# A graph block on one core: second-half one-hots made by GpSimd and ScalarE, and a transposed first layer of the experts

## The chip, the cores and the metric

The kernel runs on one NeuronCore of a Trainium2 chip. The metric is the device time of one execution in microseconds; before the change it is 5100.03 us, the median of three runs (5099.64 to 5103.68). The core's engines each work through a queue of their own in order and meet only at semaphores: TensorE (PE; its weight loads are shown as PEld), VectorE (DVE), ScalarE (ACT), GpSimd (POOL) and SyncE (SP, which here only starts DMAs).

## The reference, cut to what matters

A graph of 6250 nodes with 256 features and 106250 edges, sorted by their target node:

```
xn = layernorm(x)
h  = relu(tconv(xn));  g = tconv(h)             # two graph layers, 4 heads of 64
    tconv: kj = k[src] + e;  vj = v[src] + e;  e = edge_attr @ We
           logits = (q[dst] * kj).sum(head) / 8
           a = softmax of logits over the edges of one dst
           out = segment_sum(vj * a, dst) + x @ Ws + bs
x  = x + g + linear_attention(xn)
z  = layernorm(layernorm(x)) * gamma + beta     # the experts' own layer norm
y  = sum over the 2 best of 8 experts e: w_e * (gelu(z @ W1[e] + b1[e]) @ W2[e] + b2[e])
out = x + y                                     # W1[e]: 256x512, W2[e]: 512x256, all float32
```

## The kernel before

Stages run one after the other, with a barrier between them: `plan`, `nodes` of layer 1, `mix`, `edges` of layer 1, `nodes` and `edges` of layer 2, `finish`, `route`, `dispatch`, `experts`, `combine`. The change is in two of them.

**The edge stage.** The edges are cut into NS = 880 tiles of 128 edges, and each tile belongs to one block of 128 target nodes. T = 20 tiles make a chunk, NS / T = 44 chunks a layer; a chunk has two halves of HT = 10 tiles. Each engine has its own program over the same (chunk c, tile j), written out by hand: four chunks peeled, then a loop of ten chunks a turn. In what follows q = j // 2, since VectorE takes two tiles at once.

- SP loads the edge attributes `ea` of each tile, and the bytes `kb` from which the transposed one-hot `oht` is made.
- GpSimd (lines 859 to 870) gathers for each tile the rows of `kvD` at the edges' sources by an indirect DMA into `kv`, a ring of ten tiles. For each even j it waits first until VectorE has made the `vj` of the pair that last used these slots (`s_vj`). It also zeroes accumulator blocks (L859) and copies ten columns of indices each half chunk (L864).
- TensorE (L927, L931) computes for tile j the edge term `e` and the query of the targets (one-hot `oht` times `q`) into `ps`, four banks. After that, for the tile that lies LAG = 36 behind, it multiplies the one-hot `oh` with the weighted tile `w` into `pa` (L950). For this product it waits for `w` of the same j and for the `add` two tiles earlier. At j == 5 it transposes the logits of the chunk before (L936), at j == 13 it transposes the softmax's shifts (L941) and forms factors (L942).
- VectorE in a pair q: `add` of `pa` into the accumulator for j (L984), `kj` = kv + e (L1030), `vj` = kv + e (L1042), `add` for j + 1, `prod` = kj * query (L1062), the sum over a head (L994). At q = 2 to 5 stand the scans of the running maximum of a softmax. At q == 0 and q == 5 stands the one-hot `oh` of ten tiles, one `is_equal` of 128x1280 (L974): at q == 0 the one with m = 2c - 3 into half 1, at q == 5 the one with m = 2c - 2 into half 0. TensorE uses the latter from j == 16 of chunk c to j == 5 of chunk c + 1.
- ScalarE makes `w` for (c, j), the tile 36 behind: four scaled copies of a head (L909) and one of the weights (L911). `w` has four slots, so it runs at most four tiles ahead of TensorE's L950. Between them stand `keyed`, Abs and Relu that make `oht` from `kb` (L883, L885), at j == 4 and j == 14, and the exponentials at j == 15.

**The experts.** Nodes are sorted by expert into NE = 108 tiles of 128 rows (a multiple of 6; 105 suffice). For each tile: two transposes of x (L1499), a copy to SBUF by ScalarE (L1537), the first layer with x as the stationary operand and W1 moving, 512 columns (L1508), bias by VectorE (L1565), gelu by ScalarE (L1543), four transposes of the result (L1517), a copy by ScalarE (L1549), the second layer (L1526), bias by VectorE (L1573), a store. Each engine runs the steps of several tiles interleaved (`piped`: step (d, f) does f for the tile d turns back). The expert's number is read into a register from a table. GpSimd has nothing to do here.

Of the kernel before, what the change touches and what calls it, by code (L numbers as in the profile page):

```python
# [32 lines left out]
EX = 8  # L33
# [23 lines left out]
def sizes(n_nodes, n_edges):  # L57

    z = Record()
    z.N, z.E = n_nodes, n_edges  # L60
    z.NB = -(-n_nodes // P)
    z.NT = -(-n_edges // P)
    z.NT += -(z.NT + z.NB - 1) % 40
    z.NS = z.NT + z.NB - 1
    z.NSP = -(-z.NS // P) * P
    z.U = z.NSP // P
    z.G = z.NSP // 32
    z.NE = -(-(2 * z.NB + EX - 1) // 6) * 6
    z.UB = max(d for d in range(1, 8) if z.NB % d == 0)
    return z  # L70
# [669 lines left out]
def edges(nc, z, g, layer, a):  # L740
# [3 lines left out]
    with Stage(nc, f"edge{layer}") as st:  # L744
# [42 lines left out]
        s_resc, s_vinit, s_off, s_abs = (st.sem(n) for n in ("s_resc", "s_vinit", "s_off", "s_abs"))  # L787
# [56 lines left out]
        def _(pool):  # L844
# [32 lines left out]
        def _(act):  # L877
# [37 lines left out]
        def _(pe):  # L915
# [38 lines left out]
        def _(dve):  # L954
# [42 lines left out]
            def chunk(c, k0, u, kept, more):  # L997
# [9 lines left out]
                for q in range(HT):  # L1007
# [65 lines left out]
                    if j % HT == 0 and lagged(c, j + 6):  # L1073
                        onehot(2 * c - (3 if j < HT else 2), 1 if j < HT else 0)
# [197 lines left out]
def route(nc, z, g, a):  # L1272
# [4 lines left out]
    with Stage(nc, "route") as st:  # L1277
# [163 lines left out]
def experts(nc, z, g, a):  # L1441
# [3 lines left out]
    with Stage(nc, "exp") as st:  # L1445
        xr = st.sb("xr", [P, UE, D])
        xT = st.sb("xT", [P, 2, D])
        hb = st.sb("hb", [P, 2, HID])
        hg = st.sb("hg", [P, 2, HID])
        hT = st.sb("hT", [P, 2, HID])  # L1450
        yo = st.sb("yo", [P, UE, D])
        pX = st.ps("pX", [P, 2, 2 * D])
        pH = st.ps("pH", [P, 2, HID])
        pT = st.ps("pT", [P, 2, HID])
        pY = st.ps("pY", [P, 2, 2 * D])
        s_tx, s_xT, s_h, s_hb, s_hg, s_th, s_hT, s_y, s_yo = (
            st.sem(n) for n in ("s_tx", "s_xT", "s_h", "s_hb", "s_hg", "s_th", "s_hT", "s_y", "s_yo"))
# [5 lines left out]
        def piped(eng, stages):  # L1463
# [11 lines left out]
            for j in range(deep):  # L1475
                for d, f in stages:
                    if j < d:
                        f(n_turns - 1, j - d + UE)

        @block.sync  # L1480
        def _(sp):
            def body(i):
                for j in range(UE):
                    t = i * UE + j
                    need(sp, s_tx, t - UE + 1)
                    sp.dma_start(xr[:, j, :], g.xsD[bass.ds(t * P, P), :]).then_inc(s_x[j], 16)
            turns(sp, n_turns, body)

        @block.tensor
        def _(pe):  # L1490
# [11 lines left out]
            def first(i, j):  # L1502
                t = i * UE + j
                e = expert(t)
                pe.wait_ge(s_xT, t + 1)
                need(pe, s_hb, t - 1)
# [5 lines left out]
            def h_transpose(i, j):  # L1512
                t = i * UE + j
                pe.wait_ge(s_hg, t + 1)
                need(pe, s_hT, t - 1)
                for c in range(KH):
                    ins = nc.tensor.transpose(pT[:, j % 2, c * P:(c + 1) * P], hg[:, j % 2, c * P:(c + 1) * P], g.ident[:, :])  # L1517
                ins.then_inc(s_th, 1)
# [10 lines left out]
            piped(pe, ((0, x_transpose), (1, first), (2, h_transpose), (3, second)))  # L1529

        @block.scalar
        def _(act):
            def x_copy(i, j):
                t = i * UE + j
                act.wait_ge(s_tx, t + 1)
                need(act, s_h, t - 1)
                nc.scalar.activation(xT[:, j % 2, :], pX[:, j % 2, 0:D], ACT.Copy).then_inc(s_xT, 1)  # L1537

            def gelu(i, j):
                t = i * UE + j  # L1540
                act.wait_ge(s_hb, t + 1)
                need(act, s_th, t - 1)
                nc.scalar.activation(hg[:, j % 2, :], hb[:, j % 2, :], ACT.Gelu).then_inc(s_hg, 1)  # L1543

            def h_copy(i, j):
                t = i * UE + j
                act.wait_ge(s_th, t + 1)
                need(act, s_y, t - 1)
                nc.scalar.activation(hT[:, j % 2, :], pT[:, j % 2, :], ACT.Copy).then_inc(s_hT, 1)  # L1549
# [4 lines left out]
            piped(act, ((0, x_copy), (1, gelu), (2, h_copy), (4, store)))  # L1554
            for j in range(UE):
                act.wait_ge(s_st[j], 16 * n_turns)

        @block.vector
        def _(dve):
            def bias1(i, j):  # L1560
                t = i * UE + j
                e = dve.value_load(g.etab[0:1, bass.ds(t, 1)], min_val=0, max_val=EX - 1)
                dve.wait_ge(s_h, t + 1)
                need(dve, s_hg, t - 1)
                nc.vector.tensor_tensor(hb[:, j % 2, :], pH[:, j % 2, :], g.b1[:, bass.ds(e, 1), :].rearrange("p o n -> p (o n)"),  # L1565
                                        ALU.add).then_inc(s_hb, 1)
# [8 lines left out]
            piped(dve, ((1, bias1), (3, bias2)))  # L1575
# [70 lines left out]
def build(nc, z, a, out):  # L1646
# [24 lines left out]
    with ExitStack() as whole:  # L1671
# [28 lines left out]
        g.b1 = keep(whole, "b1", [P, EX, HID])  # L1700
# [42 lines left out]
```

## Time and profile before

| | |
|---|---|
| median of 3 runs | 5100.03 us |
| the profiled execution | 5088.28 us, its span 5086.5 us |
| PE busy | 4248.3 us, 84% |
| PEld busy | 3321.2 us, 65% |
| DVE busy | 3889.5 us, 76% |
| ACT busy | 2768.2 us, 54% |
| POOL busy | 2630.0 us, 52% |

Edge stages fill about 480 to 2150 us and 2440 to 4092 us of the span, the experts 4475 to 4920 us. Each row of a timeline gives start, duration, engine, line and operation, and in brackets how long the engine had stood idle before and who released it. Matmuls of one group are merged into one row with their count; their ends overlap the next group's start, since they are pipelined. Two float32 instructions belong to one matmul of the program.

### The profile page before, as it was taken

How to read it: one execution, taken by the hardware profiler on the slowest of the kernel's cores; microseconds unless marked ns; L12 is line 12 of the kernel's file. 1: busy time of each engine (PE TensorE's matmuls, PEld its weight loads, DVE VectorE, ACT ScalarE, POOL GpSimd, SP SyncE). 2: the span in 40 equal slices, each digit the busy share in tenths (PEclk: the TensorE clock that was granted, in tenths of full speed). 3: DMA queues.
4: the chain of work that ended last, by engine and by line, in shares of the span. 5: the costliest groups of instructions: out<-in, count | busy, mean ns of one | idle time of the engine just before them, and what ended most of it. 6: DMA issues, size and time to landing. Idle time of an engine off the chain costs nothing. (4 is left out here: it accounts for less than half of the span.)

```text
span 5086.5 us, 105694 instructions
## 1 busy us (share of the span) xinstructions
PE 4248.3 (84%) x18414; PEld 3321.2 (65%) x18415; DVE 3889.5 (76%) x8471; ACT 2768.2 (54%) x10075; POOL 2630.0 (52%) x2743
## 2 busy tenths in 40 slices
PE   2987999999999999878999999999999933089960
PEld 1555788788788788633788788788788722056640
DVE  3444999999999999944999999999999976022222
ACT  0120677777777777711577777777777721033320
POOL 1011777677677677400777767767677523600015
PEclk9998999999999999989999999999999955589985
DMA  4457877777777777444877777777777623422225
GB/s 84 137 197 218 234 218 215 210 217 216 213 214 218 209 216 220 136 138 141 253 215 218 218 210 218 217 212 215 213 216 216 169 87 139 161 67 64 64 89 153
DMA packets 617242, 923.33 MB, mean 182 GB/s; under 512 B 114469, under 2 KB 478565, under 8 KB 616390
## 3 DMA queue, kind: packets, MB, share of 16 engines
q0 software_dynamic: 154544, 502.26, 34.6%
q1 hardware_dynamic: 378822, 325.73, 22.8%
q10 hardware_dynamic: 83280, 89.03, 5.0%
q14 instruction: 422, 3.46, 0.2%
q8 instruction: 174, 2.85, 0.2%
HBM read 803.36 MB, written 113.31 MB: 180 GB/s over the span
## 5 line engine op out<-in xcount | busy, mean ns | idle before, releaser
L870 POOL DMA_INDIRECT edge_kv<-kvD,edge_ix x1760 | 1819.1, 1034 | 937.2 <-issue 431.0
L909 ACT ACTIVATE edge_w<-edge_vj,edge_ex 128x64 f32<-128x64 f32 x7040 | 1865.4, 337 | 631.9 <-PE edge_pa L950 615.7
L927 PE MATMUL edge_ps<-edge_We,edge_ea 112*128 112x256 f32 x7040 | 1838.9, 383 | 47.1 <-DVE edge_prod L1062 25.2
L927 PEld LDWEIGHTS edge_ps<-edge_We,edge_ea 112*128 112x128 f32 x7040 | 1323.9, 190 | 289.5 <-DVE edge_prod L1062 55.8
L950 PE MATMUL edge_pa<-edge_w,edge_oh 128*128 128x260 f32 x3520 | 1094.6, 393 | 116.6 <-DVE acc L984 91.4
L931 PE MATMUL edge_ps<-acc,edge_oht 128*128 x3520 | 1056.5, 381 | 0.5 <-ACT edge_oht L885 0.5
L950 PEld LDWEIGHTS edge_pa<-edge_w,edge_oh 128*128 128x128 f32 x3520 | 619.2, 189 | 316.2 <-ACT edge_w L911 177.4
L984 DVE TENSOR_TENSOR acc<-acc,edge_pa 128x260 f32 x1760 | 730.4, 415 | 91.4 <-PE edge_pa L950 45.7
L931 PEld LDWEIGHTS edge_ps<-acc,edge_oht 128*128 128x128 f32 x3520 | 674.0, 192 | 96.1 <-issue 1.9
L1030 DVE TENSOR_TENSOR edge_kj<-edge_kv,edge_ps 128x512 f32<-128x512 f32 x880 | 597.9, 679 | 39.9 <-PE edge_ps L931 20.9
L1062 DVE TENSOR_TENSOR edge_prod<-edge_kj,edge_ps 128x512 f32<-128x512 f32 x880 | 597.5, 679 | 0.0
L1042 DVE TENSOR_TENSOR edge_vj<-edge_kv,edge_ps 128x512 f32<-128x512 f32 x880 | 596.1, 677 | 0.0
L994 DVE TENSOR_REDUCE edge_Lc<-edge_prod 128x8 f32<-128x512 f32 x880 | 595.8, 677 | 0.0
L859 POOL COPY acc<-edge_zero 128x1040 f32 x440 | 469.5, 1067 | 36.6 <-DVE edge_vj L1042 32.4
L468 PE MATMUL nodes_pj<-nodes_W,nodes_xT 128*128 128x512 f32 x784 | 364.7, 610 | 26.8 <-ACT nodes_xT L409 26.8
L883 ACT ACTIVATE edge_oht<-edge_kb,edge_npart 128x1280 f32<-128x1280 uint8 x178 | 240.0, 1348 | 192.0 <-POOLq L869 104.7
L911 ACT ACTIVATE edge_w<-edge_ex 128x4 f32<-128x4 f32 x1760 | 343.4, 195 | 0.0
L1565 DVE TENSOR_TENSOR exp_hb<-exp_pH,b 128x512 f32<-128x512 f32 x108 | 74.7, 692 | 324.7 <-PE exp_pH L1508 324.7
L974 DVE TENSOR_TENSOR edge_oh<-free,relS 128x1280 f32<-128x1280 f32 x176 | 268.2, 1524 | 0.0
L468 PEld LDWEIGHTS nodes_pj<-nodes_W,nodes_xT 128*128 128x128 f32 x784 | 145.2, 195 | 182.6 <-issue 146.6
L1605 POOL COPY comb_ix<-pos 128x14 int32 (+1 forms) x7 | 1.4, 196 | 485.5 <-POOLq L86 462.0
L885 ACT ACTIVATE edge_oht<-edge_oht,ones 128x1280 f32<-128x1280 f32 x178 | 242.5, 1362 | 5.8
(230 smaller groups left out, 3140.3 us busy)
## 6 DMA issues: line engine op xcount, KB each, us to landing
edge_ea<-ea_t_dram SPq DMA_DIRECT2D x1760, 112.0 KB, 4.1
edge_kb<-relD SPq DMA_DIRECT2D x178, 160.0 KB, 4.4
edge_kv<-kvD,edge_ix POOLq DMA_INDIRECT x1760, 4.4
kvD<-nodes_kvs ACTq DMA_DIRECT2D x98, 256.0 KB, 2.1
xsD<-mix_zr POOLq DMA_DIRECT2D x27, 512.0 KB
exp_xr<-xsD SPq DMA_DIRECT2D x108, 128.0 KB, 2.0
ysD<-exp_yo ACTq DMA_DIRECT2D x108, 128.0 KB
edge_pen<-penD SPq DMA_DIRECT2D x352, 32.0 KB
```

Of the source, the lines that this page charges most:

```text
L468: ins = nc.tensor.matmul(pj[:, j % 2, n * 2 * D:(n + 1) * 2 * D], xT[:, j, c, :], W[:, c, n * 2 * D:(n + 1) * 2 * D], start=(c == 0), stop ...
L859: nc.gpsimd.tensor_copy(g.acc[:, bass.ds(block + 1, AHEAD - 1), :].rearrange("p b n -> p (b n)"), zero[:, 0:1].to_broadcast([P, (AHEAD - 1 ...
L870: nc.gpsimd.indirect_dma_start(out=kv[:, j % HT, :], out_offset=None, in_=g.kvD, in_offset=bass.IndirectOffsetOnAxis(ap=ix[:, h, j % HT:j ...
L909: nc.scalar.activation(w[:, j % 4, h * CA:h * CA + C], vj[:, slot, h * C:(h + 1) * C], ACT.Copy, scale=ex[:, x, h, k:k + 1])
L927: nc.tensor.matmul(ps[:, j % 4, 0:D], ea[:, j % HT, k, :], We[:, k, :], start=(k == 0), stop=(k == 1))
L931: nc.tensor.matmul(ps[:, j % 4, D:2 * D], oht[:, j // HT, (j % HT) * P:(j % HT + 1) * P], g.q[:, bass.ds(block, 1), 0:D].rearrange("p o d ...
L950: nc.tensor.matmul(pa[:, j % 2, 0:A], oh[:, par, (j + 4) % HT, :], w[:, j % 4, :], start=True, stop=True).then_inc(s_ape, 1)
L984: nc.vector.tensor_tensor(at, at, pa[:, j % 2, 0:A], ALU.add).then_inc(s_acc, 1)
L994: nc.vector.tensor_reduce(Lc[:, p, :, s:s + 2].rearrange("p h s -> p s h"), prod[:, q % 2, :, :].rearrange("p s (h k) -> p s h k", h=H), A ...
L1030: nc.vector.tensor_tensor(kj[:, q % 2, :, :], kv[:, both, 0:D], e, ALU.add).then_inc(s_kj, 1)
L1042: nc.vector.tensor_tensor(vj[:, p * T + j:p * T + j + 2, :], kv[:, both, D:2 * D], e, ALU.add).then_inc(s_vj, 1)
L1062: nc.vector.tensor_tensor(prod[:, q % 2, :, :], kj[:, q % 2, :, :], ps[:, bank, D:2 * D], ALU.mult).then_inc(s_prod, 1)
```

## The change

Edge stage: the one-hot with even m (half 0 of `oh`) is no longer made by VectorE. GpSimd subtracts (free index minus the edge's target, 128x1280) at j == 1 of its chunk c for m = 2c - 4, and ScalarE makes Abs and then Relu(1 - x) of it in place at j == 12 of its chunk c, for m = 2c - 2. `keyed` for the next chunk moves from j == 14 to j == 16.

Experts: the first layer is computed transposed. The W1 of the tile's expert is copied by GpSimd into `Ws` (two slots) and is the stationary operand, in blocks of 128 x 128; x transposed is moving, 128 columns. Its result has the hidden units on partitions, so the four transposes and their copy fall away, and `b1` becomes the bias of the gelu activation. The copy of x from PSUM goes from ScalarE to VectorE. NE is 105.

```diff
-    z.NE = -(-(2 * z.NB + EX - 1) // 6) * 6
+    z.NE = 2 * z.NB + EX - 1
 # edges, gpsimd
+            def offsets(m, par):
+                need(pool, s_ape, HT * m - HT)
+                nc.gpsimd.tensor_tensor(oh[:, par, :, :], g.free[:, :].unsqueeze(1).to_broadcast([P, HT, P]),
+                                        g.relS[:, bass.ds(m * HT, HT)].unsqueeze(2).to_broadcast([P, HT, P]), ALU.subtract).then_inc(s_off, 1)
             def chunk(c, k0, u, kept, more):
                 for j in range(T):
+                    if j == 1 and (not isinstance(c, int) or 2 <= c <= NCH + 1):
+                        offsets(2 * c - 4, 0)
 # edges, scalar
+            def onehot(done, par):
+                act.wait_ge(s_off, done)
+                nc.scalar.activation(oh[:, par, :, :], oh[:, par, :, :], ACT.Abs).then_inc(s_abs, 1)
+                act.wait_ge(s_abs, done)
+                nc.scalar.activation(oh[:, par, :, :], oh[:, par, :, :], ACT.Relu, bias=g.ones[:, 0:1], scale=-1.0).then_inc(s_ohs, 1)
             def chunk(c, k0, u, kept, more):
                 for j in range(T):
+                    if j == 12 and lagged(c, 16):
+                        onehot(c, 0)
-                    if j == 14 and (not isinstance(c, int) or c + 1 < NCH):
+                    if j == 16 and (not isinstance(c, int) or c + 1 < NCH):
                         keyed(2 * c + 2, c + 1, 0)
 # edges, tensor
-                            pe.wait_ge(s_oh, 2 * c - (2 if j < HT else 1))
+                            pe.wait_ge(*((s_oh, c - 1) if j < HT else (s_ohs, c)))
 # edges, vector
-                    if j % HT == 0 and lagged(c, j + 6):
-                        onehot(2 * c - (3 if j < HT else 2), 1 if j < HT else 0)
+                    if j == 0 and lagged(c, 6):
+                        onehot(2 * c - 3, 1)
 # experts, gpsimd (new)
+            def stage(i, j):
+                t = i * UE + j
+                e = pool.value_load(g.etab[0:1, bass.ds(t, 1)], min_val=0, max_val=EX - 1)
+                need(pool, s_h, t - 1)
+                nc.gpsimd.tensor_copy(Ws[:, j % 2, :, :].rearrange("p c n -> p (c n)"),
+                                      g.W1[:, bass.ds(e, 1), :, :].rearrange("p o c n -> p (o c n)")).then_inc(s_ws, 1)
 # experts, tensor, first layer
-                for c in range(2):
-                    ins = nc.tensor.matmul(pH[:, j % 2, :], xT[:, j % 2, c * P:(c + 1) * P],
-                                           g.W1[:, bass.ds(e, 1), c, :].rearrange("p o n -> p (o n)"), start=(c == 0), stop=(c == 1))
+                for m in range(KH):
+                    for c in range(2):
+                        ins = nc.tensor.matmul(pH[:, j % 2, m * P:(m + 1) * P],
+                                               Ws[:, j % 2, c, m * P:(m + 1) * P],
+                                               xT[:, j % 2, c * P:(c + 1) * P], start=(c == 0), stop=(c == 1))
-            piped(pe, ((0, x_transpose), (1, first), (2, h_transpose), (3, second)))
+            piped(pe, ((0, x_transpose), (1, first), (2, second)))
 # experts, scalar
+                for m in range(KH):
+                    ins = nc.scalar.activation(hT[:, j % 2, m * P:(m + 1) * P], pH[:, j % 2, m * P:(m + 1) * P], ACT.Gelu,
+                                               bias=g.b1[:, bass.ds(e, 1), m])
-            piped(act, ((0, x_copy), (1, gelu), (2, h_copy), (4, store)))
+            piped(act, ((1, gelu), (3, store)))
 # experts, vector
-            piped(dve, ((1, bias1), (3, bias2)))
+            piped(dve, ((0, x_copy), (2, bias2)))
```

The rest of the diff is the loading of `b1` in its new layout and the last, incomplete turn of the experts' loop.

## Rows read from the trace of the kernel before

**Rows 1.** The page: its first line.
```profile
span 5086.5 us, 105694 instructions
```

**Rows 2.** Five chunks of edge layer 2: L974 by tile (durations min/median/max, starts); busy by engine.
```profile
L974 DVE TENSOR_TENSOR edge_oh<-free,relS x11: 1478/1481/1915, 3007.7 to 3193.8; 128x1280 f32<-128x1280 f32 x11
...
3007.67:3193.80 186.13, 180.64 (x822) 150.93 (x821) 182.90 (x386) 140.48 (x531) 131.73 (x134) 1.00 0.76 216
```

**Rows 3.** Timeline of TensorE, one chunk (start us, us, engine line op).
```profile
3001.53 1.03 PE L927 MATMUL edge_ps<-edge_We,edge_ea 112*128 112x256 f32 x4
...
3010.21 1.03 PE L927 MATMUL edge_ps<-edge_We,edge_ea 112*128 112x256 f32 x4
...
3011.51 0.27 PE L936 MATMUL edge_pm<-ident,edge_Lc 128*128 128x128 f32 x1
...
3022.01 0.60 PE L931 MATMUL edge_ps<-acc,edge_oht 128*128 x2
...
3024.18 0.62 PE L950 MATMUL edge_pa<-edge_w,edge_oh 128*128 128x260 f32 x2
...
3026.05 0.28 PE L942 MATMUL edge_pm<-edge_Ym,ones 128*128 128x4 f32 x2
```

**Rows 4.** Timeline of VectorE, the same chunk: q = 0, then q = 5.
```profile
3004.95 0.68 DVE L1030 TENSOR_TENSOR edge_kj<-edge_kv,edge_ps 128x512 f32<-128x512 f32 x1
...
3023.90 0.68 DVE L1030 TENSOR_TENSOR edge_kj<-edge_kv,edge_ps 128x512 f32<-128x512 f32 x1
...
3024.83 0.68 DVE L1042 TENSOR_TENSOR edge_vj<-edge_kv,edge_ps 128x512 f32<-128x512 f32 x1
...
3027.77 1.48 DVE L974 TENSOR_TENSOR edge_oh<-free,relS 128x1280 f32<-128x1280 f32 x1
```

**Rows 5.** Timeline of ScalarE, the same chunk: j = 12 and j = 14.
```profile
3017.57 1.07 ACT L909 ACTIVATE edge_w<-edge_vj,edge_ex 128x64 f32<-128x64 f32 x4 [0.67 <-PE edge_pa L950]
...
3020.58 1.34 ACT L883 ACTIVATE edge_oht<-edge_kb,edge_npart 128x1280 f32<-128x1280 uint8 x1
3021.96 1.36 ACT L885 ACTIVATE edge_oht<-edge_oht,ones 128x1280 f32<-128x1280 f32 x1
3023.23 1.05 ACT L909 ACTIVATE edge_w<-edge_vj,edge_ex 128x64 f32<-128x64 f32 x4
```

**Rows 6.** Timeline of GpSimd: the next chunk's gather for j = 0.
```profile
3026.31 0.96 POOL L870 DMA_INDIRECT edge_kv<-kvD,edge_ix  x1 [1.59 <-DVE edge_vj L1042]
```

**Rows 7.** GpSimd's operations by line: durations in ns, min/median/max.
```profile
L1176 POOL TENSOR_TENSOR fin_xg<-fin_xn,fin_gam x49: 717/724/901, 4115.7 to 4277.3; 128x256 f32<-128x256 f32 x49
...
L859 POOL COPY acc<-edge_zero x440: 1051/1058/1704, 497.6 to 4058.0; 128x1040 f32 x147
...
L864 POOL COPY edge_ix<-srcS x176: 189/201/1521, 478.3 to 4021.2; 128x10 int32 x160, 128x10 int32<-128x10 int32 x16
```

**Rows 8.** TensorE at edge layer 1's start: timeline; a window (PE busy, clock, DMA share, GB/s).
```profile
481.71 2.05 PE L927 MATMUL edge_ps<-edge_We,edge_ea 112*128 112x256 f32 x4 [8.11 <-DMA edge_ea<-ea_t_dram]
...
485.89 0.60 PE L931 MATMUL edge_ps<-acc,edge_oht 128*128 x2
...
480.00:485.00 5.00, 3.29 (x7) 0.50 0.77 216
```

**Rows 9.** TensorE: one tile of the experts; L465's 128-column matmuls of 100 us (PE, PEld busy).
```profile
4703.63 1.88 PE L1508 MATMUL exp_pH<-W,exp_xT 128*128 x4
4705.35 0.60 PE L1517 MATMUL exp_pT<-ident,exp_hg 128*128 128x128 f32 x4
4705.79 1.89 PE L1526 MATMUL exp_pY<-W,exp_hT 128*128 x8
...
4707.73 1.88 PE L1508 MATMUL exp_pH<-W,exp_xT 128*128 x4
...
200.00:300.00 100.00, 22.40 (x168) 20.63 (x168) 1.00 0.39 132
```

**Rows 10.** ScalarE in the experts: the gelu of 512 columns.
```profile
4706.39 0.63 ACT L1543 ACTIVATE exp_hg<-exp_hb 128x512 f32<-128x512 f32 x1 [2.17 <-DVE exp_hb L1565]
```

More of the change, by code:

```diff
@@ L786, in edges @@
         s_oh, s_w, s_ape, s_acc, s_init = (st.sem(n) for n in ("s_oh", "s_w", "s_ape", "s_acc", "s_init"))
-        s_resc, s_vinit, s_off, s_abs = (st.sem(n) for n in ("s_resc", "s_vinit", "s_off", "s_abs"))
+        s_resc, s_vinit, s_off, s_abs, s_ohs = (st.sem(n) for n in ("s_resc", "s_vinit", "s_off", "s_abs", "s_ohs"))
         s_mt, s_m, s_D, s_et, s_ex, s_Y = (st.sem(n) for n in ("s_mt", "s_m", "s_D", "s_et", "s_ex", "s_Y"))
@@ L1474, in piped @@
             turns(eng, n_turns, body, peel=2)
-            for j in range(deep):
+            for t in range(n_turns * UE, NE + deep):
                 for d, f in stages:
-                    if j < d:
-                        f(n_turns - 1, j - d + UE)
+                    if t - d < NE:
+                        f((t - d) // UE, (t - d) % UE)
         @block.sync
@@ L1485, in body, with _ @@
                     need(sp, s_tx, t - UE + 1)
-                    sp.dma_start(xr[:, j, :], g.xsD[bass.ds(t * P, P), :]).then_inc(s_x[j], 16)
+                    if not isinstance(t, int) or t < NE:
+                        sp.dma_start(xr[:, j, :], g.xsD[bass.ds(t * P, P), :]).then_inc(s_x[j], 16)
             turns(sp, n_turns, body)
+            body(n_turns)
+        @block.gpsimd
+        def _(pool):
+            def stage(i, j):
[4 more added lines that the diff above has]
+                                      g.W1[:, bass.ds(e, 1), :, :].rearrange("p o c n -> p (o c n)")).then_inc(s_ws, 1)
+            piped(pool, ((0, stage),))
         @block.tensor
@@ L1503, in first @@
                 t = i * UE + j
-                e = expert(t)
                 pe.wait_ge(s_xT, t + 1)
-                need(pe, s_hb, t - 1)
-                for c in range(2):
-                    ins = nc.tensor.matmul(pH[:, j % 2, :], xT[:, j % 2, c * P:(c + 1) * P],
-                                           g.W1[:, bass.ds(e, 1), c, :].rearrange("p o n -> p (o n)"), start=(c == 0), stop=(c == 1))
-                ins.then_inc(s_h, 1)
[L1512 to L1518, printed above, removed]
+                pe.wait_ge(s_ws, t + 1)
+                need(pe, s_hT, t - 1)
+                for m in range(KH):
[3 more added lines that the diff above has]
+                                               xT[:, j % 2, c * P:(c + 1) * P], start=(c == 0), stop=(c == 1))
+                ins.then_inc(s_h, 1)
             def second(i, j):
@@ L1553, in store, with x_copy @@
                 act.dma_start(g.ysD[bass.ds((i * UE + j) * P, P), :], yo[:, j, :]).then_inc(s_st[j], 16)
-            piped(act, ((0, x_copy), (1, gelu), (2, h_copy), (4, store)))
+            piped(act, ((1, gelu), (3, store)))
             for j in range(UE):
-                act.wait_ge(s_st[j], 16 * n_turns)
+                act.wait_ge(s_st[j], 16 * -(-(NE - j) // UE))
         @block.vector
         def _(dve):
-            def bias1(i, j):
+            def x_copy(i, j):
                 t = i * UE + j
[L1562 to L1566, printed above, removed]
+                dve.wait_ge(s_tx, t + 1)
+                need(dve, s_h, t - 1)
+                nc.vector.tensor_copy(xT[:, j % 2, :], pX[:, j % 2, 0:D]).then_inc(s_xT, 1)
             def bias2(i, j):
@@ L1734 @@
         lay[n] = np.asarray(inputs["L0_ffn_" + n])
+    lay["b1_T"] = np.ascontiguousarray(lay.pop("b1").reshape(EX, HID // P, P).transpose(2, 0, 1))
     nc = bacc.Bacc("TRN2", target_bir_lowering=False, num_devices=1)
```

26 lines of the change are left out of this document (7 added, 19 removed).

## The prediction

> **What bounds the kernel now.** I read the page first: its 40 slices show two long plateaus (the edge stage of each graph layer) in which TensorE and VectorE both stand at nine tenths or more, and near the end a short stretch where TensorE alone does. The span is 5086.5 us [rows 1]. Then I asked for busy time in a stretch of exactly five chunks inside the second plateau. The `is_equal` one-hot of VectorE comes twice a chunk, and ten intervals of it take 186.1 us, so a chunk of 20 tiles takes 37.2 us; in that stretch VectorE is busy 182.90 of 186.13 us and TensorE 180.64 [rows 2]. Next come the timelines of the engines in one chunk, since shares cannot say who waits for whom.
>
> TensorE [rows 3]: from the first row to the second are 5 tiles in 8.68 us, 1.736 us a tile, 34.7 us a chunk. The transpose of `Lc` and the group at j == 13 (last row) add at most their own 0.27 and 0.28 us, together about 0.5. So TensorE alone needs 35.2 us a chunk and now loses 2.0 to waits. VectorE [rows 4]: the pairs from q = 0 to q = 5 take 3004.95 to 3023.90, 18.95 us, where TensorE needs 5 x 3.47 + 0.1 = 17.5. So VectorE falls behind by 1.5 us here and sets the pace; it makes that up in the second half of the chunk, were it not for the one-hot at q = 5, 1.48 us, which is the one the change takes away. VectorE is the bound by a thin margin, TensorE stands 2.0 us behind it.
>
> ScalarE [rows 5] makes the weighted tile `w` of a j up to four tiles before TensorE multiplies it: `w` of j = 12 starts at 3017.57 (released by TensorE's j = 8), and TensorE takes it at 3024.18 [rows 3]. GpSimd [rows 6] runs ahead too, but only by the ten slots of `kv`: its gather for j = 0 of the next chunk starts at 3026.31, after a wait for VectorE's `vj` of q = 5, which ended at 3024.83 + 0.68 = 3025.51 [rows 4].
>
> **Edit 1, the one-hot of each second half.** Removed: 1.48 us of VectorE a chunk. Added: a subtract on GpSimd (`offsets`), Abs and Relu on ScalarE (`onehot`). What decides is their place in two queues. `offsets(2c-2)` stands at j == 1 of GpSimd's chunk c+1, behind the gather of j = 0 of that chunk. ScalarE waits for that very subtract (`s_off >= c`) at j == 12 of chunk c, ahead of `w` for j = 12. TensorE needs that `w` for the product of j = 12, before it does anything else. So every chunk gets a chain, begun when `vj` of q = 5 ends (call it V):
>
> - to the start of the gather 0.80 us (3025.51 to 3026.31), the gather 0.96 [rows 4, 6];
> - the subtract, 128x1280, two SBUF inputs. The trace has none of that size. The nearest row is GpSimd's 128x256 multiply, 717 ns [rows 7]. Above: five of these, 3.6 us. Below: the rate of GpSimd's one-input copy, 1.058 us for 1040 columns, gives 1.3 us. A copy of ten columns takes 0.20, so some 0.2 of the 717 ns is fixed; (0.717 - 0.2) x 5 + 0.2 = 2.8 us. I take 2.8, as the multiply has the two inputs;
> - to ScalarE, an estimate of 0.1; Abs to Relu 1.38 (3020.58 to 3021.96), Relu to the next `w` 1.27 (to 3023.23), `w` itself 1.05 for four heads and about 0.1 for its tail [rows 5]; to TensorE an estimate of 0.1.
>
> Sum: 0.80 + 0.96 + 2.8 + 0.1 + 1.38 + 1.27 + 1.15 + 0.1 = 8.6 us after V. Meanwhile everything stops: TensorE in order at the product of j = 12; VectorE after the rest of q = 5, as `add` of j = 12 needs that product; GpSimd after two gathers, as the next need `vj` of q = 6.
>
> The new period, from one product of j = 12 to the next: TensorE's own chunk 35.2, less what lies between the end of the products of j = 11 into `ps` (3022.01 + 0.60 = 3022.61) and the product of j = 12 (3024.18) [rows 3], 1.57, makes 33.6. Add 0.2 for waits on `add` that stay (an estimate, a tenth of the 2.0 lost now, since VectorE now follows). Add the clock: where TensorE had stood 8.11 us it came back at a granted clock of 0.50, and L927, L931, L927 took 4.18 us from 481.71 to 485.89 [rows 8], against 0.87 + 0.43 + 0.87 = 2.17 at full clock [rows 3]: 2.0 lost. The stall here is longer (below), so I add 2.0. Then V after TensorE's j = 11: the lag of 1.5 us that VectorE gathers from q = 0 to q = 5, and kj to the end of `vj`, 3023.90 to 3025.51, 1.6 [rows 4]; 3.1. Then the chain, 8.6. Sum 33.6 + 0.2 + 2.0 + 3.1 + 8.6 = 47.5 us against 37.2: 10.3 more a chunk. TensorE stands 3.1 + 8.6 - 1.57 = 10.1 us in each. VectorE's saved 1.48 us buys nothing; its cover was the chunk's critical path, which has moved.
>
> That clock loss draws on one gap of the trace. The Trainium skill ("TensorE: Matmul & The Clock Gate", section "HAM oscillation — how this bites in real kernels") says that a kernel whose every loop turn has such a gap pays the slow start in every turn. By that rule the 2.0 us belongs in all chunks, without it the period is 45.5 us; only the one gap here bears it out.
>
> How often: NS / T = 44 chunks a layer. c = 2 to 42 have it in full. c = 43: GpSimd's chunk 44 has no gathers, the subtract can start some 1.2 us sooner. c = 1 has nothing queued before j = 16, and TensorE reaches that four tiles later; Relu ends 3.1 - 1.15 us or so later than needed with keyed and `w` behind it, about 3.5 us. c = 44 and the tail: nothing to gather, no stall, one one-hot less. Per layer 42 x 10.3 - 1.2 + 3.5 - 1.4 = 434, two layers +868 us.
>
> keyed moved from j == 14 to j == 16: two ScalarE activations, 2.65 us [rows 5], needed by TensorE only at j = 0 of the next chunk. After the stall ScalarE does `w` of 12 to 15 at about 1.15 us each while TensorE needs 1.74 or more, so I cost it at nothing; if that cover were gone it would cost up to 1 us a chunk.
>
> **Edit 2, the experts.** Now TensorE works without a gap, 4703.63 to 4707.73, 4.10 us a tile, 108 tiles, 443 us [rows 9]. Removed: the four transposes of `hg`, 4705.35 to 4705.79, 0.44 us; three tiles of padding, 12 us. The first layer goes from 4 instructions of 512 columns (4703.63 to 4705.35, 1.72) to 16 of 128. Groups of eight such products, with as many weight loads, stand in the node stage: 168 take 22.40 us, 21 groups of 1.067 [rows 9], in which the last product's tail is about 0.17, so 0.112 each. 16 x 0.112 = 1.79, 0.07 more. New tile 4.10 - 0.44 + 0.07 = 3.73; 105 x 3.73 = 392: -51 us. Bounds: as 16 x 0.107 it is -58; were every load exposed by as much as a product, 16 x 0.11 = 1.8 a tile, +138.
>
> Added and hidden: GpSimd's copy of the expert's weights, 1024 columns, near the 1.06 us of 1040 [rows 7], or with the multiply's rate 2.1; it has from the end of `first(t-2)` to `first(t)`, one and a half tiles, 5.5 us. ScalarE: four gelus of 128 columns in place of three activations; a 512-wide one takes 0.63 [rows 10], so four cost between 0.63 and 2.5 of the 3.73. The copy of `x` goes to VectorE, which loses `bias1`. Register loads of the expert number on GpSimd and ScalarE are not in the trace; at under 1 us they stay covered, if not the copy's cover is gone by their excess. SP's queue: the same loads, three fewer; ScalarE's stores likewise. `b1` is loaded as 4 columns an expert; the route stage ends on VectorE's chain, so nothing.
>
> **Sum.** 5088.3 (profiled execution, 5086.5 and 1.8 around) + 868 - 51 = 5905 us. The median of the runs shown is 12 us above it, which I add: 5917.
>
> **Rivals.**
> 1. No clock loss: a stall of 10 us does not lower the clock every time. 5917 - 2 x 42 x 2.0 = 5750. For it: in the long plateau the clock is 1.00. Against: the 8.11 us gap.
> 2. Not slower. The chain ends before TensorE wants `w` of j = 12, because GpSimd is further ahead than in the rows. Then VectorE's load falls to 37.2 - 1.4 = 35.8, TensorE's 35.2, and the period is some 35.6: -1.6 x 88 = -141, with the experts 5100 - 192 = 4908. It decides from a subtract that starts 10.1 us earlier, three pairs of gathers. GpSimd is idle a quarter of the time, but the ring of ten `kv` slots holds it, so the row of 3026.31 speaks against.
> 3. The experts' weight loads are exposed: 5917 + 51 + 138 = 6106. The node stage's rows speak against.
> 4. The subtract runs at the copy's rate: 1.5 us less a chunk, 5917 - 126 = 5791; inside the range.
>
> **How the numbers follow.** My case, with 4 in it: 0.83. Rival 1: 0.07. Rival 2: 0.05. Rival 3: 0.03. The rest, a stall much shorter or something unseen, 0.02. The range takes in the subtract from 1.3 to 3.6 us (-126 to +67), an error of 1 us a chunk in lag and waits (84 either way), and rival 1: 5740 to 6060. About 0.2% is what a measurement tells from no change. Faster 0.06, same 0.01, slower 0.93.
>
> **What would show it.** In the edge stage after: a period near 47.5 us; TensorE's longest wait is `pa` <- `w` of ScalarE, near 10 us, once a chunk, about 84 times; ScalarE waits for GpSimd's `oh` from about where it now starts `w` of j = 12; the subtract stands right behind a gather released by `vj`; the first L950 and L927 after each stall take twice their time and the mean granted clock of the stage falls below 0.95. In the experts TensorE stays gapless at about 3.73 us a tile. I am wrong if `offsets` starts well ahead of `vj` of q = 5, or if TensorE finds `w` of j = 12 ready.

## The result and the profile after

The changed kernel takes 5946.29 us (median of 4 runs, 5939.01 to 5950.19) against 5101.85 for the kernel before on the same chip (5099.64 to 5105.57): ratio 1.1653, 95% interval 1.1632 to 1.1673. The profiled execution took 5945.37 us. I had forecast 5917 in a range of 5740 to 6060. Medians of the kernel before differ by half a per cent from one batch of runs to the next, on the same chip too (5076.44 and 5103.20 on one of them), so the experiments are compared as ratios, each to the kernel before in its own batch.

The page of the changed kernel: span and busy time by engine, granted clock in slices, the costliest groups (busy, mean ns | idle before, releaser); line numbers in the edge stage are 7 to 15 higher than before (L859 is L866, L870 is L877, L927 is L942, L950 is L965).

```profile
span 5943.0 us, 107412 instructions
PE 4414.9 (74%) x19200; PEld 3569.5 (60%) x19201; DVE 3782.1 (64%) x8377; ACT 2890.5 (49%) x10348; POOL 2870.4 (48%) x2936
PEclk9988888888888888889888888888888887558995
L965 PE MATMUL edge_pa<-edge_w,edge_oh 128*128 128x260 f32 x3520 | 1187.3, 422 | 808.5 <-ACT edge_w L926 796.9
L897 ACT ACTIVATE edge_oh<-edge_oh 128x1280 f32<-128x1280 f32 x88 | 111.7, 1269 | 1114.9 <-POOL edge_oh L852 1114.9
```

The span is 856.5 us longer [rows 1], VectorE has 107 us less to do, and no engine is above 74%: the time is not in work but in waits. The view of waits gives the links (waited for: us in total, times, longest):

```profile
ACT edge_oh L897 <- POOL edge_oh L852: 1114.9, 86, 25.6
PE edge_pa L965 <- ACT edge_w L926: 796.9, 120, 10.6
DVE acc L999 <- PE edge_pa L965: 711.9, 256, 7.9
```

ScalarE waits for GpSimd's subtract once a chunk, TensorE for ScalarE's `w`, VectorE for TensorE's product. One chunk on the four engines, VectorE first (`vj` of q = 5, then the next `add`):

```profile
3445.53 0.68 DVE L1057 TENSOR_TENSOR edge_vj<-edge_kv,edge_ps 128x512 f32<-128x512 f32 x1
...
3455.52 0.43 DVE L999 TENSOR_TENSOR acc<-acc,edge_pa 128x260 f32 x1 [7.32 <-PE edge_pa L965]
```

GpSimd, ending with the subtract:

```profile
3447.02 0.96 POOL L877 DMA_INDIRECT edge_kv<-kvD,edge_ix  x1 [1.59 <-DVE edge_vj L1057]
3448.00 2.34 POOL L852 TENSOR_TENSOR edge_oh<-free,relS 128x1280 f32<-128x1280 f32 x1
```

ScalarE, from the last `w` before the wait to the next:

```profile
3437.58 0.19 ACT L926 ACTIVATE edge_w<-edge_ex 128x4 f32<-128x4 f32 x1
3450.37 1.27 ACT L897 ACTIVATE edge_oh<-edge_oh 128x1280 f32<-128x1280 f32 x1 [12.60 <-POOL edge_oh L852]
3451.67 1.36 ACT L899 ACTIVATE edge_oh<-edge_oh,ones 128x1280 f32<-128x1280 f32 x1
3452.94 1.05 ACT L924 ACTIVATE edge_w<-edge_vj,edge_ex 128x64 f32<-128x64 f32 x4
```

TensorE: the last products into `ps` of j = 12, the product of j = 12 after its wait, and what follows.

```profile
3442.72 0.60 PE L946 MATMUL edge_ps<-acc,edge_oht 128*128 x2
...
3444.45 0.60 PE L946 MATMUL edge_ps<-acc,edge_oht 128*128 x2
3454.14 1.24 PE L965 MATMUL edge_pa<-edge_w,edge_oh 128*128 128x260 f32 x2 [9.09 <-ACT edge_w L926]
3455.16 1.91 PE L942 MATMUL edge_ps<-edge_We,edge_ea 112*128 112x256 f32 x4
```

`vj` ends at 3446.21, and the product starts at 3454.14: 7.93 us, in the order gather, subtract, Abs, Relu, `w`, as the arrows name them. After the wait L965 and the four matmuls of L942 take about twice what they take elsewhere (0.60 and 1.03): from 3454 to 3458 us the granted clock is 0.50, the lower of the two levels. It is so behind each of the 86 waits of this kind (medians 1.24 and 1.91). In the kernel before, GpSimd's same gather [rows 6] was followed at once by the next one (at 3027.58), and TensorE had its `w`.

The stages, by the start of their first instruction: the edge stage of layer 1 with the node stage behind it takes 2389.4 us (471.8 to 2861.2) where it took 1930.2 (477.2 to 2407.4), 459 more; the edge stage of layer 2 takes 2142.1 for 1687.7, 454 more; the experts take 402.7 for 452.5, 49.8 less. One tile of the experts, in the changed kernel (before: [rows 9]):

```profile
5600.76 1.95 PE L1533 MATMUL exp_pH<-exp_xT,exp_Ws 128*128 128x128 f32 x16
5602.54 1.89 PE L1544 MATMUL exp_pY<-W,exp_hT 128*128 x8
5604.27 0.38 PE L1523 MATMUL exp_pX<-ident,exp_xr 128*128 128x128 f32 x2
5604.49 1.73 PE L1533 MATMUL exp_pH<-exp_xT,exp_Ws 128*128 128x128 f32 x14
```

TensorE is gapless there, 3.73 us a tile.

### The profile page after: what moved, and what is told of

Read it like the earlier page. It is cut to its first block and busy times, and to the rows that moved or that the text cites. A ratio compares the mean times of both kernels' runs of the same rounds, so it can differ in the third digit from the quotient of the medians.

```text
span 5943.0 us, 107412 instructions
## 1 busy us (share of the span) xinstructions
PE 4414.9 (74%) x19200; PEld 3569.5 (60%) x19201; DVE 3782.1 (64%) x8377; ACT 2890.5 (49%) x10348; POOL 2870.4 (48%) x2936
## 3 DMA queue, kind: packets, MB, share of 16 engines
q14 instruction: 424, 3.47, 0.2%
## 5 line engine op out<-in xcount | busy, mean ns | idle before, releaser
L877 POOL DMA_INDIRECT edge_kv<-kvD,edge_ix x1760 | 1754.3, 997 | 1701.8 <-DVE edge_vj L1057 1208.7
L942 PE MATMUL edge_ps<-edge_We,edge_ea 112*128 112x256 f32 x7040 | 1933.9, 399 | 44.8 <-DVE edge_prod L1077 20.4
L965 PE MATMUL edge_pa<-edge_w,edge_oh 128*128 128x260 f32 x3520 | 1187.3, 422 | 808.5 <-ACT edge_w L926 796.9
L942 PEld LDWEIGHTS edge_ps<-edge_We,edge_ea 112*128 112x128 f32 x7040 | 1414.6, 202 | 309.2 <-issue 48.0
L965 PEld LDWEIGHTS edge_pa<-edge_w,edge_oh 128*128 128x128 f32 x3520 | 672.7, 203 | 985.9 <-ACT edge_w L926 849.2
L946 PE MATMUL edge_ps<-acc,edge_oht 128*128 x3520 | 1096.8, 393 | 0.5 <-issue 0.5
L946 PEld LDWEIGHTS edge_ps<-acc,edge_oht 128*128 128x128 f32 x3520 | 699.4, 199 | 107.5 <-issue 1.8
L897 ACT ACTIVATE edge_oh<-edge_oh 128x1280 f32<-128x1280 f32 x88 | 111.7, 1269 | 1114.9 <-POOL edge_oh L852 1114.9
L866 POOL COPY acc<-edge_zero 128x1040 f32 x440 | 467.0, 1061 | 46.1 <-DVE edge_vj L1057 41.9
L1557 ACT ACTIVATE exp_hT<-exp_pH,b 128x128 f32<-128x128 f32 x420 | 119.8, 368 | 267.4 <-PE exp_pH L1533 267.4
L1509 POOL COPY exp_Ws<-W 128x1024 f32 x105 | 109.2, 1040 | 289.8 <-PE exp_pH L1533 278.5
```

Source lines behind the costliest of these rows:

```text
L866: nc.gpsimd.tensor_copy(g.acc[:, bass.ds(block + 1, AHEAD - 1), :].rearrange("p b n -> p (b n)"), zero[:, 0:1].to_broadcast([P, (AHEAD - 1 ...
L877: nc.gpsimd.indirect_dma_start(out=kv[:, j % HT, :], out_offset=None, in_=g.kvD, in_offset=bass.IndirectOffsetOnAxis(ap=ix[:, h, j % HT:j ...
L942: nc.tensor.matmul(ps[:, j % 4, 0:D], ea[:, j % HT, k, :], We[:, k, :], start=(k == 0), stop=(k == 1))
L946: nc.tensor.matmul(ps[:, j % 4, D:2 * D], oht[:, j // HT, (j % HT) * P:(j % HT + 1) * P], g.q[:, bass.ds(block, 1), 0:D].rearrange("p o d ...
L965: nc.tensor.matmul(pa[:, j % 2, 0:A], oh[:, par, (j + 4) % HT, :], w[:, j % 4, :], start=True, stop=True).then_inc(s_ape, 1)
```

## The experiments

Period means the median of the 43 distances between two chunks' groups of j == 13 on TensorE in layer 1 (before: 37.07 us; changed kernel: 47.76). All kernels are the changed one with the edit shown.

| run | what it is | ratio to before | 95% | period |
|---|---|---|---|---|
| e1_edges_only | experts as before | 1.1794 | 1.1774 to 1.1813 | 47.71 |
| e2_experts_only | edge stage as before | 0.9912 | 0.9896 to 0.9929 | 37.05 |
| e10_experts_again | the same, again | 0.9898 | 0.9884 to 0.9912 | 37.06 |
| e3_scalar_at_16 | Abs and Relu at j == 16 | 1.005 | 1.0034 to 1.0067 | 37.50 |
| e5b_filler | 20 products in the wait | 1.128 | 1.1264 to 1.1296 | 44.95 |
| e6_subtract_twice | subtract doubled | 1.2013 | 1.1993 to 1.2033 | 49.79 |
| e8_copy_twice | copy of W1 doubled | one run, 5948.19 us | | 47.76 |
| e4_subtract_early | subtract at j == 15 | 0.9921 | 0.9903 to 0.9939 | 36.75 |
| e7_subtract_at_14 | subtract at j == 14 | 0.9888 | 0.987 to 0.9906 | 37.10 |
| e9_subtract_17_scalar_13 | subtract at 17, Abs at 13 | 1.0056 | 1.0044 to 1.0068 | 38.29 |
| e11_first_half | the other one-hot | 0.9932 | 0.9918 to 0.9945 | 36.86 |
| e12_first_half_6 | the same, subtract at j == 6 | 0.9821 | 0.9804 to 0.9838 | 36.44 |

### Which part costs

e1_edges_only takes back every experts hunk of the diff. 

> The edge edits alone, the experts as before. My theory: the loss is all in the edge stage, the experts give about 50 us back, so this is slower than the full change by 50: 5946 + 50 = 5996 us, ratio 1.175. The period of a chunk stays 47.4 to 47.8 us. Rival: the experts' edit costs something elsewhere (the weight loads, the copy on GpSimd) and the edges lose less; then this kernel is at or below 5946.

e2_experts_only takes back every edge-stage hunk. 

> The experts' edits alone, the edge stage as before. My theory: 5102 - 50 = 5052 us, ratio 0.990; the tile takes 3.74 us as in the changed kernel, 105 tiles. Rival: the two edits interact over the stage boundary (buffers, barriers), then this and the edges alone do not add up to the full change within 10 us.

Measured 1.1794 and 0.9912. Their effects add up nearly: 1.1794 + 0.9912 - 1 = 1.1706 against 1.1653, 0.5% apart, which is more than the intervals. The two batches differ by as much in the kernel before (5076.44 and 5101.85 us), and the changed kernel was not run in the first one; so whether the gap is one of batches or of the kernel stays open. The edge part costs the whole loss, the experts gain what was forecast.

### Is it the place in ScalarE's queue

```diff
-                    if j == 12 and lagged(c, 16):
-                        onehot(c, 0)
-                    if j == 16 and (not isinstance(c, int) or c + 1 < NCH):
+                    if j == 14 and (not isinstance(c, int) or c + 1 < NCH):
                         keyed(2 * c + 2, c + 1, 0)
+                    if j == 16 and lagged(c, 16):
+                        onehot(c, 0)
```

> The full change, but ScalarE's Abs and Relu stand at j == 16, right before TensorE needs that one-hot, and keyed stands at j == 14 as before. Theory A (the queue: w of j = 12 to 15 stands behind the wait for GpSimd): GpSimd's subtract still ends about 4.1 us after vj of q = 5, Relu 2.65 later, w of 16 at 7.9, TensorE is there at about 6.0, so a stall of about 2 us a chunk is left instead of 9.1, and with it the clock loss goes: period 37.2 to 38, total 5050 to 5120 us. Theory B (the chain from GpSimd is too late for TensorE in itself, whatever stands behind it; or the extra work on ScalarE and GpSimd is what costs): the period stays above 44 us and the total above 5600.

Measured 1.005, period 37.5. All the instructions of the change are still there, at the same lengths; only their order in ScalarE's queue is another: `w` of j = 12 to 15, `keyed` and the exponentials now stand ahead of the wait. Of the 796.9 us that TensorE waited for `w`, 149.9 are left, and of ScalarE's 1114.9 us 174.0. So the loss is the order of ScalarE's queue against GpSimd's, not the work moved.

### Two sizes of the chain: the clock and the subtract

```diff
+                        if j == 12:
+                            need(pe, s_ex, c - 1)
+                            for _ in range(20):
+                                nc.tensor.matmul(pm[:, 1, D + 8:2 * D], g.ident[0:EP, :], We[:, 0, 0:D - 8], start=True, stop=True)
```

> The full change, and TensorE, before it waits for w of j = 12, does 20 float32 products of 248 columns into an unused part of a PSUM bank (about 8.3 us of the 9.1 us stall; nothing uses their result). My theory, clock: in the stall the granted clock falls to 0.50, and the work after it loses 2.6 us a chunk. With the filler the clock stays 1.00, the first products after the stall take 0.6 us and not 1.24, the period falls from 47.7 to about 45.1, and the total by 86 x 2.6 = 224 us: ratio 1.165 - 0.044 = 1.121. Rival: the clock after the stall does not matter since VectorE or ScalarE sets the pace there: within 30 us of the changed kernel, ratio 1.16, or slower by what the filler overruns.

Measured 1.128. TensorE's timeline in it (the filler, then the product of j = 12):

```profile
3420.48 8.53 PE L965 MATMUL edge_pm<-edge_We,ident 112*128 112x248 f32 x40
3429.73 0.70 PE L969 MATMUL edge_pa<-edge_w,edge_oh 128*128 128x260 f32 x2 [0.72 <-ACT edge_w L926]
3430.28 1.03 PE L942 MATMUL edge_ps<-edge_We,edge_ea 112*128 112x256 f32 x4
```

The useless products fill the wait and 0.72 us of it remain; L942 takes 1.03 again where it took 1.91. From the end of `vj` of q = 5 to TensorE's product it is 7.93 us in both kernels (medians), so the chain is the same. The period falls by 47.76 - 44.95 = 2.8 us, and that is about what the clock cost in each chunk: a kernel that does more work is 3% faster. The Trainium skill ("TensorE: Matmul & The Clock Gate", section "HAM oscillation — how this bites in real kernels") says that a gap in each loop turn makes each turn pay the slow start; the trace agrees, with L942 at 1.91 us behind all 86 waits.

```diff
             def offsets(m, par):
                 need(pool, s_ape, HT * m - HT)
+                nc.gpsimd.tensor_tensor(spare[:, :, :], ...the same inputs..., ALU.subtract).then_inc(s_step, 1)
```

> The full change with a second GpSimd subtract of the same size into a spare tile, ahead of the real one. My theory: it lies on the chain that sets the period, so its 2.34 us come out in full, once a chunk: +2.34 to 2.45 x 85 = +200 us, 6145 us. Rival: GpSimd's own time is hidden and the stall has another cause (ScalarE's load, the clock): less than +50 us.

Measured 1.2013, 0.036 over the changed kernel, which is 183 us or 2.1 us in each of 88 chunks (the period: 2.03). The chain from `vj` to the product grows from 7.93 to 10.20 us: the second subtract of 2.34 us lands on the path nearly in full.

### The cover of the experts' copy

```diff
+                need(pool, s_wx, t)
+                nc.gpsimd.tensor_copy(Wx[:, :], g.W1[:, bass.ds(e, 1), :, :].rearrange("p o c n -> p (o c n)")).then_inc(s_wx, 1)
```

> The full change with GpSimd's copy of the expert's weights made twice, first into a spare tile. My theory: the copy is hidden, GpSimd stands idle 2.69 of 3.74 us a tile, so a second 1.04 us changes nothing: the tile stays 3.74 us, the experts' stage within 3 us. Rival: the copy is on the path, +1.04 us a tile, +109 us.

GpSimd does both copies in a tile (1.04 us each), and still waits for TensorE:

```profile
5602.90 1.04 POOL L1512 COPY exp_Wx<-W 128x1024 f32 x1 [1.71 <-PE exp_pH L1537]
5603.88 1.04 POOL L1513 COPY exp_Ws<-W 128x1024 f32 x1
```

The stage takes 402.7 us as in the changed kernel. The copy is hidden with room for another.

### Can the edge part pay

If the subtract starts early enough, the chain is off the path and rival 2's period, some 35.6 us, should come. Three runs tried the place:

```diff
-                    if j == 1 and (not isinstance(c, int) or 2 <= c <= NCH + 1):
-                        offsets(2 * c - 4, 0)
+                    if j == 15 and (not isinstance(c, int) or 1 <= c <= NCH):
+                        offsets(2 * c - 2, 0)
```

> The full change, but GpSimd does the subtract at j == 15 of chunk c, six tiles earlier in its queue than j == 1 of chunk c + 1; ScalarE stays at j == 12. Theory A (order in GpSimd's queue behind a gather released by vj of q = 5): the subtract now ends near the point at which ScalarE reaches j = 12, with w up to four tiles ahead, so nothing stalls; the chunk is bound by VectorE's 35.8 and TensorE's 35.2, period 35.8 to 36.4, against 37.1 before; total 5052 - 88 x (0.7 to 1.3) = 4940 to 4990 us, faster than both kernels. Theory B (the added 2.6 us of ScalarE and 2.3 of GpSimd a chunk cost by themselves, by delayed w or gathers): no better than 5052.

Measured 0.9921, period 36.75: missed, and no better than the experts alone. The stall is gone, but VectorE has a new long instruction. GpSimd, VectorE in the same stretch, then that scan over the whole run (ns, min/median/max):

```profile
3017.78 2.33 POOL L852 TENSOR_TENSOR edge_oh<-free,relS 128x1280 f32<-128x1280 f32 x1
```

```profile
3018.96 1.22 DVE L1053 TENSOR_TENSOR_SCAN edge_X<-edge_wp,edge_R,edge_TT 128x20 f32<-128x20 f32 x1
...
L1053 DVE TENSOR_TENSOR_SCAN edge_X<-edge_wp,edge_R,edge_TT x88: 253/1218/2922, 524.6 to 4062.7; 128x20 f32<-128x20 f32 x88
```

Before, the same scan took 255 ns. It ends at 3020.18, as the subtract does (3020.11): VectorE's instruction with two inputs in SBUF is held while GpSimd's runs, whereas `kj`, one of whose inputs is in PSUM, keeps its 0.68 us. So I moved the subtract one tile forward (`j == 14` for `j == 15`):

> As the subtract at j == 15, but one gather sooner, at j == 14. At j == 15 the period came out at 36.74 us: the subtract lay from 3017.78 to 3020.11, and VectorE's small scan at q = 3, both of whose inputs are in SBUF, took 1.22 us from 3018.96 instead of 0.26 and so ended with the subtract. Theory A (GpSimd's subtract holds what VectorE needs for an operation with two SBUF inputs): at j == 14 it ends near 16.8, before the scan, which takes 0.26 again; VectorE has 0.96 us a chunk less, period 35.8 to 36.0 us, total about 85 x 0.8 = 65 us under that of j == 15, ratio 0.977 to 0.982. Theory B (the period of 36.7 is set by something else, TensorE's add waits or ScalarE's extra work): period 36.6 to 36.8, ratio 0.992.

Measured 0.9888. The scan's median is 255 ns again, as expected, and the period is not below 37: missed, so the scan alone did not hold it. What VectorE waits for in five chunks of layer 2:

```profile
DVE edge_kj L1045 <- PE edge_ps L946: 7.0, 5, 1.7
```

In e2_experts_only this wait does not occur in that stretch. One of the five waits stands before q = 9, two before q = 8, two before q = 5; over the 82 full chunks of the run a wait of over 0.3 us stands before q = 8 in 30 and before q = 5 in 30. The third place was j == 17, with `onehot` on ScalarE at j == 13:

> The full change with GpSimd's subtract at j == 17 of chunk c and ScalarE's Abs and Relu at j == 13. From the trace of the subtract at j == 15: the subtract would lie from about 21.3 to 23.6 (the scan of q = 3 with two SBUF inputs is at 19.0, the next such scan at 26.0), Relu ends near 26.3, w of j = 13 near 27.5, and TensorE wants it at 29.1: no stall, no held scan, gathers 14 to 17 not delayed. Theory A (the two places were the only costs): period 35.8 to 36.2 us, 60 to 80 us under the experts' edits alone, ratio 0.976 to 0.981. Theory B (a third cost, which took the gain at j == 14: a gather that lands late once a subtract has held up GpSimd's queue): period 36.5 to 37, ratio 0.987 to 0.992.

Measured 1.0056: missed, by what looks like e4's reason again. GpSimd's zeroing COPY, pushed back by the subtract, now meets another of VectorE's scans with SBUF inputs (GpSimd and VectorE in one chunk, then the scan over the run):

```profile
3054.95 1.06 POOL L866 COPY acc<-edge_zero 128x1040 f32 x1
```

```profile
3054.84 1.46 DVE L1092 TENSOR_TENSOR_SCAN edge_B<-edge_pen,edge_GY,edge_F 128x128 f32<-128x128 f32 x1
...
L1092 DVE TENSOR_TENSOR_SCAN edge_B<-edge_pen,edge_GY,edge_F x88: 472/1460/1804, 530.3 to 4160.3; 128x128 f32<-128x128 f32 x88
```

It took 475 ns in the kernel before. How much of this run's 1.2 us a chunk over the kernel before the scan explains (1.0) rests on its length alone; no run separates it. The table further down shows the rest: beside the 1.0 of the scan, at q = 4, the pair of q = 7 is 1.4 us longer, by a wait for `ps`, which is all that the pair of q = 5 had saved. The control for e7:

> The experts' edits alone, run again beside the one above so that the two are compared on the same chip: ratio 0.990, period 37.05 us. Nothing else is asked of it.

Its interval overlaps that of e7, so up to here nothing showed a gain from the edge part.

### Where the saved time has to lie

e7 saves VectorE 1.4 us a chunk, and in that stretch of layer 2 VectorE waits 1.4 us a chunk for `ps`. That gave a new theory: VectorE falls behind TensorE from q = 0 to q = 5 (the scans) and catches up after that, 3.06 us a pair against 3.47. The one-hot of q = 5 stood where it catches up. Without it VectorE only catches up sooner, and waits. I had put all five waits before q = 8, where this holds; two stand before q = 5, and for those the theory has no reason. By it the one to take away is the other, at q = 0:

```diff
-                        offsets(2 * c - 4, 0)          # GpSimd, j == 1
+                        offsets(2 * c - 3, 1)          # GpSimd, j == 4
-                        onehot(c, 0)                   # ScalarE, j == 12; keyed at 4 and 16
+                        onehot(c - 1, 1)               # ScalarE, j == 2; keyed at 6 and 14
-                        onehot(2 * c - 3, 1)           # VectorE, q == 0
+                        onehot(2 * c - 2, 0)           # VectorE, q == 5
```

> The other one-hot is taken from VectorE: GpSimd and ScalarE make the one of odd m (subtract at j == 4 of GpSimd's chunk, Abs and Relu at j == 2 of ScalarE's, keyed back at 14 and its neighbour from 4 to 6); VectorE keeps the one of even m, at q == 5. The experts are as in the changed kernel. VectorE loses the same 1.48 us a chunk as in e7_subtract_at_14, but in the half in which it falls behind TensorE. Theory S (only what is saved while VectorE is behind counts; in the second half of a chunk it catches up with TensorE and then waits for ps, as the 7.0 us in five chunks before kj of q = 8 show in e7): the period falls by a further 0.9 to 1.4 us below the 36.9 of e7, to 35.5 to 36.0, no wait of VectorE before kj at q = 8, time 0.965 to 0.974 of the kernel before. Theory L (the saved load counts wherever it stands, and something else holds e7): 36.7 to 37.0 and 0.987 to 0.992, as e7. If the chain reaches TensorE here as in the changed kernel, TensorE stalls before j = 6 and the time is above 1.0.

Measured 0.9932, period 36.86: neither theory's numbers. The wait at q = 8 is gone, but one instruction of q = 7 with both inputs in SBUF has grown, as it runs beside the subtract:

```profile
L1036 DVE TENSOR_TENSOR acc<-acc,edge_fn x88: 410/1176/1778, 540.3 to 4077.6; 128x260 f32 x88
```

The last run moves the subtract two tiles on, to j == 6, and Abs and Relu to j == 4:

> e11_first_half with the subtract at j == 6 of GpSimd's chunk in place of j == 4 and ScalarE's Abs and Relu at j == 4 in place of j == 2, so that VectorE's acc <- acc, fn at q = 7 (both inputs in SBUF; it takes 1.165 us on average in e11, where the subtract runs beside it, and 0.416 in e2_experts_only) no longer meets the subtract. Theory P (what holds e11 at 36.86 us a chunk is this one instruction, since VectorE's intervals otherwise sum to 35.8): its mean falls to 0.42 to 0.5 us, the period to 35.9 to 36.3, time 0.978 to 0.985 of the kernel before. Theory W (VectorE's lost time is made up by waits elsewhere, TensorE's product order sets the period): the instruction is short again and the period stays at 36.7 to 37.0, 0.990 to 0.994.

Measured 0.9821, inside what theory P expected; the period, 36.44, is 0.1 above its range. GpSimd, VectorE in one chunk, and that instruction over the run:

```profile
3038.12 2.34 POOL L852 TENSOR_TENSOR edge_oh<-free,relS 128x1280 f32<-128x1280 f32 x1
```

```profile
3036.56 0.42 DVE L1036 TENSOR_TENSOR acc<-acc,edge_fn 128x260 f32 x1
...
L1036 DVE TENSOR_TENSOR acc<-acc,edge_fn x88: 413/421/1911, 536.6 to 4022.0; 128x260 f32 x88
```

The subtract starts after the `add` has ended, and meets no such instruction. This is the fastest of the kernels here: 4990.04 us against 5077.51, 0.8 to 0.9% below the experts alone (0.9898 and 0.9912). The distances from `kj` of one pair to the next on VectorE, medians over layer 1, worked out from the traces, show where the time goes:

```
from q =                    0     1     2     3     4     5     6     7     8     9
e2_experts_only           4.46  3.06  4.09  3.54  3.80  5.24  3.06  3.67  3.06  3.06
changed kernel            4.47  3.06  4.10  3.54  3.80 13.37  4.94  3.69  3.26  3.47
e7_subtract_at_14         4.46  3.06  4.10  3.55  3.83  3.84  3.06  3.87  3.06  3.06
e9_subtract_17_scalar_13  4.46  3.06  4.10  3.54  4.80  3.84  3.06  5.08  3.06  3.06
e11_first_half            3.08  3.47  4.10  3.54  3.80  5.24  3.06  4.43  3.06  3.06
e12_first_half_6          3.29  3.47  4.10  3.54  3.80  5.25  3.06  3.68  3.06  3.06
```

In e12 1.17 us are saved at q = 0, and 0.41 of them are lost at q = 1, where VectorE has caught up with TensorE and waits for `ps`. The theory of the place is in keeping with e12 against e7: the same 1.48 us taken from VectorE, 36.44 against 37.10. The two also differ in where the subtract stands, and that part was not tried alone, so the place is argued and not shown.

## Why the prediction was right, step by step

It was right in mechanism and close in size; the expected gain of the edge part, 1.48 us of VectorE, could not show since the path ran past it.

- **The chain.** 8.6 us forecast from V to TensorE's product, 7.93 measured. Of the difference 0.46 is the subtract, 2.34 us where I scaled the 256-column multiply to 2.8. Its price per column is below what 717 ns less 0.2 fixed gives; rival 4's 1.3 was further off. The gather started 0.81 after V (0.80 forecast) and took 0.96. e3 shows that the chain is the cause, e6 that a microsecond in it is nearly one of the chunk (2.27 and 2.03).
- **The lag of VectorE.** 3.1 us from TensorE's j = 11 to V, 2.89 measured (3443.32 to 3446.21).
- **The clock.** I added 2.0 us from the one gap before; 2.8 by e5b. The stretch from 3454.14 on holds it: L965 1.24 for 0.60, L942 1.91 for 1.03, and the slow matmuls run on to 3459.2. Rival 1, no clock loss, is out; its price was too small by 0.8 a chunk. This error and those of the chain (0.67) and the lag (0.2) nearly cancel, which is luck. The mean granted clock of the two edge stages is 0.89, below the 0.95 that the prediction gave as a sign; in the kernel before it was 0.99 (layer 1).
- **The stall.** 10.1 forecast, 9.1 measured, by the shorter chain and lag (0.9).
- **The period.** 47.5 forecast, 47.76 measured; against 37.2 and 37.07 that is +10.3 and +10.7 a chunk. With the lag, the chain and the clock as measured, 34.1 us are left for TensorE's own work and its other waits, for which the sum had 33.8.
- **How often.** TensorE has 86 waits of over 3 us before this product, for my 84 to 86. The two ends of a layer were poor estimates: the first wait (c = 1), costed at about 3.5, is 7.07 in layer 1 and 10.32 in layer 2; the last (c = 43), costed at 10.1 less 1.2, is 6.3. Over the stages +459 and +454 came for 434 each. By the medians 42 x 0.4 = 17 of the 20 to 25 missing are the period; the rest was not divided further.
- **The whole.** For the profiled execution the sum had 868 - 51 = +817 us, and +857 came (5088.28 to 5945.37). The forecast of 5917 is nearer to its median, since it has 12 us added because the profiled execution before lay that far under the median; the one after lies 1 us under. That too is luck.
- **keyed at j == 16.** Costed at nothing. It was not tried alone; e3, which moves it back and `onehot` behind it, does not separate the two.
- **The experts.** -51 forecast, -49.8 in the stage, and 0.9898 and 0.9912 (45 to 52 us) alone. The tile is 3.73 as forecast; its first layer of 16 products takes 1.78 (5600.76 to 5602.54) for my 1.79: the weight loads are hidden, and rival 3 is out. The copy is hidden (e8), with 1.71 us of GpSimd's wait left after a second one.
- **Rival 2.** It asked for a subtract 10.1 us earlier and promised a period of 35.6, which is already below the 35.8 that it gives for VectorE alone. e4 and e7 granted the condition, and the stall went, but 36.75 and 37.10 came, not 35.6. Its price was wrong in two ways that the sum over VectorE's load could not show: the held scan (e4, e7), and, as argued above, the place of the saving, in the half where VectorE catches up. Taking the other one-hot away and keeping GpSimd off VectorE's SBUF instructions gives 36.44: 0.63 of the 1.47 us between 37.07 and 35.6.

What stays open: e7's own loss is only partly accounted for. Over both layers VectorE stood 84.2 us before `kj` for TensorE's `ps` (77 times), against 26.9 (17 times) in e2_experts_only, of some 88 x 1.4 = 123 saved. As many of these waits stand before q = 5 as before q = 8, and the theory of the place does not say why one should stand at q = 5. Nor is it known why the two parts do not add up exactly.

## What to carry to other kernels

An operation moved to another engine costs by where it stands in that engine's queue: write down for each in-order queue what stands ahead of the new instruction and what is queued behind the wait for it, before counting its work. Ask too where the busiest engine is behind its partner: relief there paid here (e12), while the same relief where it catches up came back as a wait (e9, and in part e7). And a stall of TensorE costs more than its length: here 9.1 us of standing cost 2.8 more in clock.

## What the runs showed of the hardware

- GpSimd's 128x1280 subtract of two broadcast SBUF inputs takes 2.34 us, the 128x256 multiply 0.717: 1.58 ns a column between them ((2338 - 717) / 1024), against about 1.0 for the copy (1.04 us for 1024 columns).
- While it runs, VectorE's instructions with two inputs that both lie in SBUF wait: a scan of 20 columns 0.255 to 1.22 us (e4), the `add` of 260 columns 0.42 to 1.18 (e11). GpSimd's zeroing copy did the same to a scan of 128 columns, 0.475 to 1.46 (e9). Those that read PSUM beside SBUF kept their 0.68 (`kj`, `vj`, `prod`), and so did the sum over a head, whose one input lies in SBUF: 0.68 beside the subtract in 84 chunks of e12. The Trainium skill ("SBUF — State Buffer", section "Who interferes with whom") says that GpSimd and VectorE share one port pair as an exclusive lock, and that an instruction of VectorE with two SBUF inputs contends with one of GpSimd that reads SBUF, one with a single SBUF input not; the runs agree on both.
- It goes the other way too: in the changed kernel a gather's DMA_INDIRECT that began at 3428.61 took 2.08 us, not 0.96, while VectorE made its one-hot (1.48 us from 3428.37). Of the 1760 gathers 82 began inside a one-hot, with a median of 2.08 us; the others have a median of 0.95, and none of them took over 1.5.
